# A new order of the same 1519 steps in a one-core chain of four convolution blocks

## Chip, cores and metric

The kernel runs on one core of a Trainium2 chip. The metric is the device time of one execution in microseconds (us); lower is better. Besides TensorE (PE), VectorE (DVE), ScalarE (ACT), GpSimd (POOL) and SyncE (SP) the core has 16 DMA engines.

## What is computed

Four blocks follow each other on an input x of 4 images, 512 channels, 32x32 pixels, all in fp32:

```
# L0: deformable bottleneck
out    = relu(bn1(conv1x1(x)))                     # 512 -> 128
offset = conv3x3(out) + off_b                      # 18 values for each pixel
out    = relu(bn2(deform_conv3x3(out, offset)))    # 9 taps, 4 corners each, bilinear
x      = relu(bn3(conv1x1(out)) + x)               # 128 -> 512
# L1: local self correlation, 5x5 window, normalised, beside x
gs     = l2norm(sum_c x[y+dy, x+dx] * x[y, x])     # 25 values for each pixel
x      = relu(W @ concat(x, gs) + b)
# L2, L3: two residual bottlenecks (1x1 to 128, 3x3, 1x1 to 512, plus x, relu)
```

## The kernel before

**Tiling.** An image has 1024 pixels. It is worked in two halves `h` of 512 pixels, which is one bank of PSUM, and the 512 channels in four groups `m` of 128. The deformable convolution of one image is 18 units `u` (2 halves x 9 taps). A unit has 4 tiles of 128 pixels and is cut in two parts `q` of two tiles.

**The path of a unit.** `gather.i.u.q` issues two indirect DMAs on POOL (L572), each of which fetches for 128 pixels the four corner pixels (128 x 512 floats, 256 KB) from a table in HBM into one of 12 `patch` slots. Behind each DMA POOL waits for its own last `tick` and adds a single number to itself (L577); this is the pause behind each gather. `weigh` (ACT, L860) multiplies the first corner, `blend` (DVE, L1130) adds the other three in six instructions, `turn` (PE, L694) transposes the four tiles, `sampT` (ACT, L868) copies them out of PSUM, and `tap` (PE, L705) multiplies by the weights of the tap. A gather may only start when the blend of three units before has emptied its slots. After nine taps come `hid` (ACT), four `out0` (PE, L713), and `xsum`, `xhigh`, `xlow` (DVE, ACT, DVE), which make the sum with x, and its split into a high and a low part. `res` on SP loads x for `xsum` into two buffers.

**What goes before.** `conv1`, `mid`, `taps`, `tapped`, `shift` and `positions` make the offsets, the addresses and the weights of an image; `midT`, `pixels` and `table` write its table. `stage`, `split`, `splitlow`, `scale`, `turnw`, `w3turn`, `w3scale` and their like prepare the weights of the later blocks.

**What comes behind.** L1 is `gram` (PE, 24 matmuls of 256 columns), `copies` (ACT), `win`, `norm` (DVE), `corrT` (PE, L732), `gsT`, `gslow`, `mixA` and `mixB` (PE, L749), `mixhigh`, `mixlow`. L2 and L3 (the third number of a step is 2 or 3) are `red`, `cvA` and `cvB`, `ex`, each followed by a `val`, a `high` (ACT) and a `low` (DVE) step, and at the end `final` and `store`. These matmuls are made as three products each (L596 to L598, the function `product`).

**What sets the order.** The string `ORDER` lists all steps. Every engine walks it from the front, and issues the steps that are its own, in this order and no other. All waits are counted from it too: `nth(step)` is how often a kind has been reached, and a wait is always for the number that its producer has in the string. `assign` walks the same string to give five PSUM banks (`take` waits until the last user has returned one) and four `ring` slots. So a moved step changes the place of its instructions on its engine, and, with the banks, what a later step waits for, but not what it computes. An order keeps `turn`s of image 3 among the L2 and L3 matmuls of image 2, and so on; behind `turn.3.17`, the last, only image 3's own L1, L2 and L3 and what is left of image 2 are to be done.

Of the kernel before, what the change touches and what calls it, by code (L numbers as in the profile page):

```python
# [1238 lines left out]
```

## Time and profile before

| | |
|---|---|
| median of three runs | 678.51 us (675.9 to 679.7) |
| the profiled execution | 670.66 us, span of its core 668.9 us |
| busy: PE, DVE, POOL, ACT | 586.6, 436.1, 400.1, 321.5 us |
| mean granted TensorE clock | 0.949 |
| moved by DMA | 110.07 MB, 75.52 MB of it by the gathers |

The span is the time from the first to the last instruction of the core. A busy time is the sum of what the records of an engine cover. Matmuls of PE overlap each other, so that the sum of their durations is more than the time they take; the time that a step takes is read from the distance of starts. "Granted clock" is the share of full speed (2.4 GHz) that TensorE was given; it is either 1.0 or 0.5 (1.2 GHz) at a time.

### The profile page before, as it was taken

How to read it: one execution, taken by the hardware profiler on the slowest of the kernel's cores; microseconds unless marked ns; L12 is line 12 of the kernel's file. 1: busy time of each engine (PE TensorE's matmuls, PEld its weight loads, DVE VectorE, ACT ScalarE, POOL GpSimd, SP SyncE). 2: the span in 40 equal slices, each digit the busy share in tenths (PEclk: the TensorE clock that was granted, in tenths of full speed). 3: DMA queues.
4: the chain of work that ended last, by engine and by line, in shares of the span. 5: the costliest groups of instructions: out<-in, count | busy, mean ns of one | idle time of the engine just before them, and what ended most of it. 6: DMA issues, size and time to landing. Idle time of an engine off the chain costs nothing.

```text
span 668.9 us, 8597 instructions
## 1 busy us (share of the span) xinstructions
PE 586.6 (88%) x2568; PEld 427.8 (64%) x2568; DVE 436.1 (65%) x1288; ACT 321.5 (48%) x702; POOL 400.1 (60%) x598
## 2 busy tenths in 40 slices
PE   6966876346979899999999899997999899999997
PEld 2654563133767677657777675574877675888776
DVE  3236668576869688788894765894876577473222
ACT  2233445434445476554542864643356745423533
POOL 2287757888684787886878486875269851000000
PEclk9978979658889999999999999996999999999999
DMA  8797963875552655785656358764054645200003
GB/s 290 239 361 248 317 175 111 236 235 142 158 164 88 177 162 170 247 267 193 175 145 189 90 159 266 235 219 144 27 162 127 172 129 172 63 1 1 0 1 125
DMA packets 47984, 110.07 MB, mean 165 GB/s; under 512 B 7607, under 2 KB 15863, under 8 KB 47810
## 3 DMA queue, kind: packets, MB, share of 16 engines
q0 software_dynamic: 23040, 75.52, 38.0%
q1 hardware_dynamic: 24898, 34.00, 15.2%
q8 instruction: 21, 0.34, 0.2%
q14 instruction: 25, 0.20, 0.1%
HBM read 96.94 MB, written 12.55 MB: 164 GB/s over the span
## 4 chain that ended last, share of the span: by engine, by line
PE 44%; DVE 17%; POOL 12%; DMA 8%; issue 8%; ACT 6%; another core or an unknown queue 4%; SPq 0%; ACTq 0%; DVEq 0%; POOLq 0%
PE bank L596 10%; PE bank L598 10%; PE bank L597 9%; DVE samp L1130 9%; POOL patch L572 9%; PE bank L705 4%; POOL tick L577 3%; PE bank L630 3%; PE bank L779 2%; DMA res<-in_x 2%; DMA patch<-patch_table,idx_all 2%; DMA patch<-patch_tables,idx_all 2%; PE bank L694 2%; PE bank L713 1%
## 5 line engine op out<-in xcount | busy, mean ns | idle before, releaser
L572 POOL DMA_INDIRECT patch<-patch_tables,idx_all x216 | 234.5, 1086 | 94.3 <-DVE samp L1130 63.5
L1130 DVE SCALAR_TENSOR_TENSOR samp<-patch,wgt_all,samp 128x128 f32<-128x128 f32 x864 | 236.7, 345 | 72.9 <-ACT samp L860 57.8
L860 ACT ACTIVATE samp<-patch,wgt_all 128x128 f32<-128x128 f32 x288 | 98.1, 394 | 86.3 <-PE bank L694 36.5
L572 POOL DMA_INDIRECT patch<-patch_table,idx_all x72 | 74.2, 1030 | 49.3 <-DVE idx_all L1037 24.1
L577 POOL TENSOR_TENSOR tick<-tick 1x1 f32<-1x1 f32 x288 | 85.6, 297 | 5.3
L705 PE MATMUL bank<-sampT,w 128*128 128x512 f32 x144 | 77.4, 640 | 8.3 <-ACT sampT L868 5.9
L694 PE MATMUL bank<-ident_r,samp 128*128 128x128 f32 x288 | 45.8, 286 | 27.1 <-DVE samp L1130 24.3
L694 PEld LDWEIGHTS bank<-ident_r,samp 128*128 128x128 f32 x288 | 35.8, 146 | 48.7 <-DVE samp L1130 34.9
L596 PE MATMUL bank<-x_high,l1w_high 128*128 128x512 f32 x128 | 55.5, 434 | 0.1
L868 ACT ACTIVATE sampT<-bank 128x512 f32<-128x512 f32 x72 | 42.0, 589 | 23.8 <-PE bank L694 11.5
L598 PE MATMUL bank<-x_high,l1w_low 128*128 128x512 f32 x128 | 50.7, 396 | 0.0
L597 PE MATMUL bank<-x_low,l1w_high 128*128 128x512 f32 x128 | 50.6, 396 | 0.0
L596 PE MATMUL bank<-x_high 128*128 128x256 f32 x128 | 40.1, 314 | 7.9 <-issue 6.1
L705 PEld LDWEIGHTS bank<-sampT,w 128*128 128x128 f32 x144 | 26.6, 204 | 26.0 <-issue 15.1
L598 PE MATMUL bank<-x_high,x_low 128*128 128x256 f32 x128 | 38.0, 297 | 2.1 <-issue 2.0
L1136 DVE SCALAR_TENSOR_TENSOR res<-bank,prm,res 128x512 f32<-128x512 f32 x32 | 23.6, 746 | 24.6 <-DMA res<-in_x 12.6
L713 PE MATMUL bank<-hid,w 128*128 128x512 f32 x64 | 34.4, 643 | 5.9 <-issue 3.3
L879 ACT ACTIVATE x_high<-res 128x512 fp32r<-128x512 f32 x32 | 20.0, 627 | 40.4 <-DVE res L1136 34.9
L597 PE MATMUL bank<-x_low,x_high 128*128 128x256 f32 x128 | 38.0, 297 | 0.3 <-issue 0.3
L630 PE MATMUL bank<-xa,w 128*128 128x512 f32 x64 | 32.5, 658 | 6.0 <-DMA xa<-in_x 6.0
L893 ACT ACTIVATE corr<-bank 32x320 f32<-32x320 f32 x64 | 27.4, 428 | 20.0 <-remote 11.1
L779 PE MATMUL bank<-xs_high,ident_r 128*128 128x512 f32 x64 | 32.1, 501 | 4.7 <-DVE h_low L1172 3.9
(178 smaller groups left out, 1165.0 us busy)
## 6 DMA issues: line engine op xcount, KB each, us to landing
res<-in_x SPq DMA_DIRECT2D x32, 256.0 KB
out_y<-ring SPq DMA_DIRECT2D x32, 256.0 KB
xa<-in_x SPq DMA_DIRECT2D x7, 1024.0 KB, 5.4
patch<-patch_tables,idx_all POOLq DMA_INDIRECT x216
patch_tables<-midT SPq DMA_DIRECT2D x11, 256.0 KB
patch<-patch_table,idx_all POOLq DMA_INDIRECT x72
xa<-in_x SPq DMA_DIRECT2D x4, 256.0 KB, 5.7
xa<-in_l1wt SPq DMA_DIRECT2D x1, 1024.0 KB
```

Source lines behind the costliest of these rows:

```text
L572: pool.indirect_dma_start(patch[:, n % SLOTS].rearrange("p a c -> p (a c)"), None, patches_n if i else patches_0, bass.IndirectOffsetOnAxi ...
L577: pool.tensor_tensor(tick[:, 1:2], tick[:, 0:1], tick[:, 0:1], ALU.add).then_inc(ticked, 1)
L596: pe.matmul(ps, w[0], a[0], start=start, stop=False)
L597: pe.matmul(ps, w[0], a[1], start=False, stop=False)
L598: return pe.matmul(ps, w[1], a[0], start=False, stop=stop)
L630: last = pe.matmul(ps[:], w1[:, c, :], xa[i % 2][:, c, h * HALF:(h + 1) * HALF], start=c == 0, stop=c == KC - 1)
L694: last = pe.transpose(bank[TURN_BANK + u % 2][:, t * P:(t + 1) * P], samp[:, u % 2, t, :], ident)
L705: pe.matmul(bank[TAP_BANK][:], w2[:, k, :], sampT[:, u % 2, :], start=k == 0, stop=k == TAPS - 1).then_inc(tap_done, 1)
L779: pe.matmul(ps[:], ident_r[:], xs[p][:, m, h * HALF:(h + 1) * HALF], start=p == 0, stop=False)
L860: act.activation(samp[:, u % 2, t, :], patch[:, g % SLOTS, 0, :], ACT.Copy, scale=wgt_all[:, i, (HT * h + t) * TAPS + k, 0:1]).then_inc(we ...
L868: act.activation(sampT[:, u % 2, :], bank[TURN_BANK + u % 2][:], ACT.Copy).then_inc(sampT_done, 1)
L1130: dve.scalar_tensor_tensor(o_, g_, w_, o_, ALU.mult, ALU.add).then_inc(blended, 1)
```

## The change

The string `ORDER` is replaced by another order of the same 1519 steps. No other line is changed: no instruction is added or removed, and the pause behind each gather is there before and after. Of the steps in their engines' sequences, 55 of 412 of PE, 54 of 383 of DVE, 68 of 501 of ACT and 138 of 145 of POOL stand at the same place. Below are both orders from the front to `turn.0.17`, and both places of `turn.3.17`.

```diff
-shift.0 table.0.1 midT.0.0 positions.0 conv1.1.0 pixels.0.0 table.0.0 mid.1.0 gather.0.0.0 taps.1.0 xload.2.0
-conv1.1.1 midT.1.0 gather.0.0.1 mid.1.1 gather.0.1.0 tapped.1.0 midT.1.1 taps.1.1 taps.1.2 gather.0.1.1 xload.2.1
-tapped.1.1 weigh.0.1.0 pixels.1.0 weigh.0.0.0 blend.0.0.0 blend.0.1.0 gather.0.2.0 conv1.2.0 mid.2.0 tapped.1.2
-pixels.1.1 gather.0.2.1 midT.2.0 shift.1 weigh.0.0.1 weigh.0.1.1 blend.0.0.1 blend.0.1.1 pixels.2.0 xload.3.0
-res.0.0.0 gather.0.3.0 positions.1 turn.0.0 taps.2.0 weigh.0.2.1 sampT.0.0 tapped.2.0 gather.0.3.1 conv1.2.1 xload.3.1
-gather.0.4.0 tap.0.0 weigh.0.2.0 mid.2.1 taps.2.1 midT.2.1 turn.0.1 weigh.0.3.0 gather.0.4.1 blend.0.2.0 blend.0.3.0
-blend.0.2.1 turn.0.2 gather.0.5.0 conv1.3.1 table.1.1 stage.0 table.2.0 weigh.0.4.0 gather.0.5.1 weigh.0.3.1 sampT.0.1
-blend.0.4.0 blend.0.3.1 tap.0.1 turn.0.3 gather.0.6.0 weigh.0.5.0 blend.0.5.0 w3turn w3scale sampT.0.2 pixels.2.1
-sampT.0.3 gather.0.6.1 conv1.3.0 w3back tap.0.2 weigh.0.5.1 weigh.0.4.1 blend.0.5.1 blend.0.4.1 scale.0 gather.0.7.0
-w3s scale.1 tap.0.3 turn.0.4 turn.0.5 sampT.0.4 weigh.0.6.1 tapped.2.1 gather.0.7.1 taps.2.2 tapped.2.2 weigh.0.7.0
-weigh.0.6.0 shift.2 blend.0.6.1 blend.0.6.0 table.1.0 stage.1 res.0.0.1 split.2 mid.3.0 gather.0.8.0 mid.3.1
-gather.0.8.1 positions.2 taps.3.0 turn.0.6 taps.3.1 turnw.1 taps.3.2 tap.0.4 gather.0.9.0 weigh.0.8.0 sampT.0.5
-tap.0.5 tapped.3.2 split.1 sampT.0.6 tapped.3.1 blend.0.8.0 gather.0.9.1 blend.0.7.0 tapped.3.0 weigh.0.8.1
-weigh.0.7.1 turnw.0 tap.0.6 shift.3 midT.3.0 split.4 blend.0.8.1 blend.0.7.1 gather.0.10.0 positions.3 gather.0.10.1
-turn.0.7 weigh.0.9.1 weigh.0.9.0 sampT.0.7 turn.0.8 tap.0.7 sampT.0.8 gather.0.11.0 tap.0.8 pixels.3.0 split.5
-blend.0.9.1 blend.0.9.0 weigh.0.10.1 gather.0.11.1 split.3 hid.0.0 weigh.0.10.0 blend.0.10.1 blend.0.10.0 out0.0.0.0
-gather.0.12.0 out0.0.0.1 turn.0.9 xsum.0.0.1 weigh.0.11.0 sampT.0.9 splitlow.3 xsum.0.0.0 gather.0.12.1 xhigh.0.0.1
-out0.0.0.3 tap.0.9 midT.3.1 turn.0.10 blend.0.11.0 xlow.0.0.1 gather.0.13.0 res.0.0.3 table.3.0 sampT.0.10
-weigh.0.12.0 blend.0.12.0 corrw xhigh.0.0.0 out0.0.0.2 weigh.0.11.1 gather.0.13.1 weigh.0.12.1 pixels.3.1 split.0
-blend.0.11.1 splitlow.4 xsum.0.0.3 splitlow.0 xlow.0.0.0 blend.0.12.1 gather.0.14.0 turn.0.11 res.0.0.2 table.3.1
-table.2.1 sampT.0.11 weigh.0.13.1 xsum.0.0.2 splitlow.1 gather.0.14.1 tap.0.10 turn.0.12 xhigh.0.0.3 weigh.0.14.0
-weigh.0.13.0 split.6 blend.0.13.1 gather.0.15.0 blend.0.13.0 xhigh.0.0.2 xlow.0.0.2 xlow.0.0.3 tap.0.11 turn.0.13
-splitlow.6 blend.0.14.0 splitlow.5 gather.0.15.1 weigh.0.14.1 weigh.0.15.0 gather.0.16.0 blend.0.15.0 res.0.1.1
-gram.0.0 res.0.1.0 gather.0.16.1 blend.0.14.1 sampT.0.13 sampT.0.12 weigh.0.15.1 blend.0.15.1 gather.0.17.0 tap.0.12
-tap.0.13 turn.0.14 splitlow.2 turn.0.15 weigh.0.16.1 sampT.0.14 gather.0.17.1 sampT.0.15 weigh.0.16.0 blend.0.16.1
-blend.0.16.0 tap.0.14 tap.0.15 weigh.0.17.0 mixA.0.0.0 gather.1.0.0 blend.0.17.0 weigh.0.17.1 turn.0.16 blend.0.17.1
-gather.1.0.1 sampT.0.16 tap.0.16 turn.0.17 sampT.0.17 weigh.1.0.0 tap.0.17 gather.1.1.0 blend.1.0.0 hid.0.1 out0.0.1.0
...
-weigh.3.17.1 sampT.3.14 tap.3.13 final.2.1.0 turn.3.16 tap.3.14 sampT.3.15 blend.3.17.1 store.2.1.0 tap.3.15
-sampT.3.16 xlow.3.0.3 turn.3.17 tap.3.16 sampT.3.17 res.3.1.1 res.3.1.0 tap.3.17 ex.2.3.1.3 hid.3.1 out0.3.1.1
-final.2.1.3 out0.3.1.0 store.2.1.3 xsum.3.1.1 ex.2.3.1.1 xhigh.3.1.1 xsum.3.1.0 xlow.3.1.1 xhigh.3.1.0 out0.3.1.3
...
+shift.0 table.0.1 midT.0.0 positions.0 pixels.0.0 table.0.0 gather.0.0.0 xload.2.0 conv1.1.1 gather.0.0.1 conv1.1.0
+gather.0.1.0 xload.2.1 conv1.2.0 gather.0.1.1 weigh.0.0.1 mid.1.1 mid.1.0 weigh.0.0.0 taps.1.0 blend.0.0.0
+gather.0.2.0 taps.1.2 midT.1.0 taps.1.1 blend.0.0.1 gather.0.2.1 weigh.0.1.1 tapped.1.1 tapped.1.0 turn.0.0 conv1.2.1
+tapped.1.2 pixels.1.0 xload.3.0 table.1.0 weigh.0.1.0 gather.0.3.0 blend.0.1.1 blend.0.1.0 weigh.0.2.0 midT.1.1
+turn.0.1 shift.1 gather.0.3.1 blend.0.2.0 sampT.0.0 mid.2.0 weigh.0.2.1 mid.2.1 blend.0.2.1 gather.0.4.0 taps.2.2
+taps.2.1 tap.0.0 midT.2.1 positions.1 xload.3.1 turn.0.2 gather.0.4.1 pixels.1.1 tapped.2.1 weigh.0.3.1 pixels.2.1
+sampT.0.2 weigh.0.3.0 gather.0.5.0 blend.0.3.0 blend.0.3.1 conv1.3.0 gather.0.5.1 weigh.0.4.0 weigh.0.4.1 sampT.0.1
+blend.0.4.1 blend.0.4.0 turn.0.3 tap.0.1 taps.2.0 gather.0.6.0 sampT.0.3 weigh.0.5.1 weigh.0.5.0 tapped.2.0 midT.2.0
+turn.0.4 conv1.3.1 gather.0.6.1 tapped.2.2 mid.3.0 gather.0.7.0 blend.0.5.0 blend.0.5.1 tap.0.2 shift.2 w3turn
+turn.0.5 weigh.0.6.1 mid.3.1 gather.0.7.1 sampT.0.4 taps.3.1 taps.3.2 gather.0.8.0 res.0.0.0 stage.0 stage.1 table.1.1
+pixels.2.0 weigh.0.6.0 blend.0.6.0 blend.0.6.1 taps.3.0 turn.0.6 positions.2 res.0.0.1 gather.0.8.1 tap.0.3
+weigh.0.7.1 weigh.0.7.0 w3scale weigh.0.8.0 gather.0.9.0 weigh.0.8.1 split.5 sampT.0.5 blend.0.7.0 tapped.3.2
+gather.0.9.1 blend.0.7.1 split.3 tap.0.4 turn.0.7 gather.0.10.0 tap.0.5 blend.0.8.0 weigh.0.9.1 sampT.0.6 tapped.3.1
+split.2 gather.0.10.1 splitlow.5 blend.0.8.1 tapped.3.0 weigh.0.9.0 w3back turn.0.8 shift.3 midT.3.1 gather.0.11.0
+blend.0.9.1 scale.0 blend.0.9.0 sampT.0.7 weigh.0.10.0 gather.0.11.1 weigh.0.10.1 turn.0.9 tap.0.6 tap.0.7 sampT.0.8
+weigh.0.11.1 blend.0.10.1 turnw.0 gather.0.12.0 weigh.0.11.0 w3s blend.0.10.0 turn.0.10 midT.3.0 tap.0.8 positions.3
+gather.0.12.1 sampT.0.9 hid.0.0 weigh.0.12.0 gather.0.13.0 weigh.0.12.1 blend.0.11.1 blend.0.11.0 out0.0.0.0
+out0.0.0.1 blend.0.12.0 gather.0.13.1 corrw sampT.0.10 xsum.0.0.1 blend.0.12.1 gather.0.14.0 turn.0.11 tap.0.9
+xsum.0.0.0 scale.1 out0.0.0.3 out0.0.0.2 gather.0.14.1 xhigh.0.0.0 turn.0.12 tap.0.10 xlow.0.0.0 pixels.3.1
+xhigh.0.0.1 split.0 weigh.0.13.0 blend.0.13.0 res.0.0.2 sampT.0.11 weigh.0.13.1 gather.0.15.0 weigh.0.14.1
+weigh.0.14.0 xlow.0.0.1 blend.0.13.1 tap.0.11 turn.0.13 blend.0.14.0 xsum.0.0.2 table.2.0 res.0.0.3 gather.0.15.1
+xhigh.0.0.2 split.4 weigh.0.15.0 gather.0.16.0 xsum.0.0.3 sampT.0.12 sampT.0.13 tap.0.12 blend.0.14.1 pixels.3.0
+weigh.0.15.1 table.3.0 gather.0.16.1 blend.0.15.0 xlow.0.0.2 tap.0.13 turn.0.14 table.3.1 table.2.1 splitlow.4
+blend.0.15.1 gather.0.17.0 turn.0.15 turnw.1 sampT.0.14 weigh.0.16.1 weigh.0.16.0 gather.0.17.1 blend.0.16.1
+blend.0.16.0 sampT.0.15 turn.0.16 tap.0.14 tap.0.15 xhigh.0.0.3 split.1 weigh.0.17.0 splitlow.1 blend.0.17.0
+gather.1.0.0 split.6 weigh.0.17.1 blend.0.17.1 gather.1.0.1 sampT.0.16 corrlow splitlow.0 turn.0.17 tap.0.16
...
+sampT.3.14 weigh.3.16.1 xsum.3.0.2 xhigh.3.0.3 sampT.3.15 weigh.3.17.1 blend.3.16.1 weigh.3.17.0 cvB.2.3.0
+blend.3.17.1 blend.3.17.0 cvB.2.3.1 turn.3.17 cvval.2.3.0 turn.3.16 cvhigh.2.3.0 tap.3.14 cvlow.2.3.0 xlow.3.0.3
+tap.3.15 cvval.2.3.1 ex.2.3.0.0 cvhigh.2.3.1 cvlow.2.3.1 ex.2.3.0.2 xhigh.3.0.2 sampT.3.16 tap.3.16 sampT.3.17
...
```

## Rows read from the trace of the kernel before

**Rows 1.** The page: span, and busy time with share and instructions of each engine.
```profile
span 668.9 us, 8597 instructions
PE 586.6 (88%) x2568; PEld 427.8 (64%) x2568; DVE 436.1 (65%) x1288; ACT 321.5 (48%) x702; POOL 400.1 (60%) x598
```

**Rows 2.** Stretches: length, PE, PEld, DVE, ACT, POOL busy, clock, DMA, GB/s.
```profile
28.70:162.20 133.50, 87.05 (x362) 57.98 (x361) 87.02 (x297) 54.29 (x128) 106.19 (x151) 0.83 0.74 235
162.20:564.00 401.80, 377.19 (x1659) 276.79 (x1658) 299.37 (x869) 219.32 (x493) 290.14 (x428) 0.97 0.56 169
564.00:668.90 104.90, 100.75 (x466) 79.81 (x464) 39.39 (x68) 39.69 (x70) 0.00 (x0) 1.00 0.10 36
```

**Rows 3.** Timeline (start, us, what, idle before) of PE: two turns.
```profile
123.69 1.11 PE L694 MATMUL bank<-ident_r,samp 128*128 128x128 f32 x4 [6.54 <-DVE samp L1130]
...
563.13 0.66 PE L694 MATMUL bank<-ident_r,samp 128*128 128x128 f32 x4
```

**Rows 4.** Timeline of PE: two products of 512 columns, and `corrT.0.0`.
```profile
435.84 0.40 PE L596 MATMUL bank<-x_high,l1w_high 128*128 128x512 f32 x1
436.08 0.39 PE L597 MATMUL bank<-x_low,l1w_high 128*128 128x512 f32 x1
...
195.77 0.92 PE L732 MATMUL bank<-ident_r,gs 128*96 128x128 f32 x4 [3.42 <-issue]
```

**Rows 5.** Chain of work that ended last: a landing, and two taps.
```profile
35.55 6.19 DMA patch<-patch_table,idx_all
...
513.77 1.72 PE bank L705 x4
```

**Rows 6.** Timeline of POOL: gathers, and one slow tick.
```profile
28.75 1.14 POOL L572 DMA_INDIRECT patch<-patch_table,idx_all  x1 [24.11 <-DVE idx_all L1037]
...
66.36 0.97 POOL L572 DMA_INDIRECT patch<-patch_table,idx_all  x1
...
110.44 3.72 POOL L572 DMA_INDIRECT patch<-patch_table,idx_all  x1 [2.31 <-DVE samp L1130]
...
125.75 0.97 POOL L572 DMA_INDIRECT patch<-patch_table,idx_all  x1
127.07 0.97 POOL L572 DMA_INDIRECT patch<-patch_table,idx_all  x1
...
148.64 4.51 POOL L577 TENSOR_TENSOR tick<-tick 1x1 f32<-1x1 f32 x1
...
554.02 0.97 POOL L572 DMA_INDIRECT patch<-patch_tables,idx_all  x1
```

**Rows 7.** Timeline of DVE: the first four blends; first and last instruction of `positions.1`.
```profile
43.16 6.41 DVE L1130 SCALAR_TENSOR_TENSOR samp<-patch,wgt_all,samp 128x128 f32<-128x128 f32 x24 [15.30 <-ACT samp L860]
...
50.83 0.31 DVE L1012 TENSOR_TENSOR pos<-bank,offb_t 128x144 f32<-128x144 f32 x1 [1.26 <-PE bank L664]
...
55.71 0.38 DVE L1037 TENSOR_SCALAR idx_all<-entry 128x72 int32<-128x72 f32 x1
```

**Rows 8.** Groups of DVE: `splitlow.6`, `xlow` (count, busy us, mean ns, idle).
```profile
L1109 DVE TENSOR_TENSOR l1w_low<-xa,l1w_high 128x2048 fp32r<-128x2048 f32 x1 | 2.3, 2285 | 0.0
L1143 DVE SCALAR_TENSOR_TENSOR x_low<-res,x_high 128x512 fp32r<-128x512 f32 x32 | 21.8, 688 | 7.2 <-ACT x_high L879 6.8
```

**Rows 9.** Waits: who waited for whom, us in total, times, longest.
```profile
POOL patch L572 <- DVE samp L1130: 79.2, 24, 17.9
...
ACT samp L860 <- PE bank L694: 36.5, 14, 7.6
```

**Rows 10.** Timeline of PE, ACT and DVE: pauses without a releaser on the core.
```profile
452.69 0.28 PE L598 MATMUL bank<-x_high,x_low 128*128 128x256 f32 x1 [0.96 <-issue]
...
369.51 0.78 ACT L928 ACTIVATE ring<-bank,bn 128x512 f32<-128x512 f32 x1 [10.53 <-remote]
...
415.04 0.75 DVE L1136 SCALAR_TENSOR_TENSOR res<-bank,prm,res 128x512 f32<-128x512 f32 x1 [6.44 <-remote]
```

**Rows 11.** Busy time of the stretch around the first (columns as in rows 2).
```profile
447.00:462.00 15.00, 10.76 (x61) 9.10 (x59) 9.33 (x25) 4.49 (x12) 13.32 (x22) 0.78 0.75 227
```

More of the change, by code:

```diff
@@ new lines @@
+weigh.1.0.1 gram.0.0 gather.1.1.1 blend.1.0.0 hid.0.1 blend.1.0.1 weigh.1.1.0 gather.1.2.0 out0.0.1.1 out0.0.1.0
+blend.1.1.0 out0.0.1.2 turn.1.0 gather.1.2.1 out0.0.1.3 xsum.0.1.1 xhigh.0.1.1 xsum.0.1.0 xlow.0.1.1 xhigh.0.1.0
+sampT.1.0 res.0.1.3 xlow.0.1.0 gather.1.3.0 weigh.1.2.0 weigh.1.1.1 res.0.1.2 blend.1.1.1 mixA.0.0.3 mixA.0.0.0
+weigh.1.2.1 xsum.0.1.3 gather.1.3.1 xhigh.0.1.3 xsum.0.1.2 tap.1.0 xlow.0.1.3 xhigh.0.1.2 turn.1.1 res.1.0.1
+xlow.0.1.2 blend.1.2.1 blend.1.2.0 borders gram.0.1 res.1.0.0 weigh.1.3.0 weigh.1.3.1 gather.1.4.0 copies.0.0
@@ new lines @@
+blend.2.1.0 res.1.1.0 gram.1.0 cvval.0.3.1 gather.2.3.0 hid.1.1 weigh.2.2.0 cvhigh.0.3.1 blend.2.1.1 cvlow.0.3.1
+weigh.2.2.1 ex.0.3.0.0 out0.1.1.0 blend.2.2.1 gather.2.3.1 out0.1.1.1 copies.1.0 blend.2.2.0 ex.0.3.1.3 ex.0.3.1.0
+final.0.0.0 sampT.2.0 gather.2.4.0 xsum.1.1.0 store.0.0.0 xsum.1.1.1 xhigh.1.1.0 turn.2.2 ex.0.3.1.1 xlow.1.1.0
+xhigh.1.1.1 final.0.1.3 res.1.1.2 out0.1.1.2 turn.2.1 xlow.1.1.1 gather.2.4.1 store.0.1.3 final.0.1.0 res.1.1.3
+out0.1.1.3 store.0.1.0 final.0.1.1 tap.2.0 ex.0.3.1.2 mixA.1.0.1 weigh.2.4.0 store.0.1.1 sampT.2.1 xsum.1.1.2
@@ new lines @@
+gather.2.5.0 xhigh.1.1.2 weigh.2.3.0 xsum.1.1.3 xlow.1.1.2 xhigh.1.1.3 weigh.2.4.1 xlow.1.1.3 gather.2.5.1 weigh.2.3.1
+res.2.0.0 res.2.0.1 gram.1.1 final.0.1.2 store.0.1.2 gram.1.2 blend.2.4.0 blend.2.3.0 blend.2.3.1 blend.2.4.1
+gather.2.6.0 copies.1.1 turn.2.3 mixA.1.0.3 gram.1.3 win.1.0.0 win.1.0.1 gather.2.6.1 copies.1.2 weigh.2.5.0
+weigh.2.5.1 win.1.0.2 mixA.1.0.0 win.1.0.3 gather.2.7.0 root.1.0 copies.1.3 sampT.2.2 norm.1.0 gather.2.7.1
+blend.2.5.0 corrT.1.0 tap.2.1 win.1.1.0 mixA.1.0.2 win.1.1.1 gather.2.8.0 gsT.1.0 gslow.1.0 mixB.1.0.0 mixB.1.0.1
@@ new lines @@
+final.1.1.3 res.2.1.2 sampT.3.0 xlow.2.1.1 store.1.1.3 blend.3.2.0 res.2.1.3 mixA.2.0.3 gather.3.5.0 xsum.2.1.2
+xhigh.2.1.2 xsum.2.1.3 turn.3.2 xlow.2.1.2 xhigh.2.1.3 weigh.3.3.0 tap.3.0 gather.3.5.1 res.3.0.0 xlow.2.1.3 tap.3.1
+blend.3.3.0 gram.2.1 weigh.3.4.0 weigh.3.3.1 blend.3.4.0 gather.3.6.0 weigh.3.4.1 copies.2.0 blend.3.3.1 gram.2.2
+blend.3.4.1 gather.3.6.1 copies.2.1 turn.3.3 gram.2.3 win.2.0.0 gather.3.7.0 win.2.0.1 sampT.3.3 copies.2.2 sampT.3.2
+win.2.0.2 mixA.2.0.0 mixA.2.0.2 win.2.0.3 gather.3.7.1 root.2.0 copies.2.3 norm.2.0 win.2.1.0 weigh.3.5.0 corrT.2.0
```

225 lines of the change are left out of this document (103 added, 122 removed).

## Prediction

> **What bounds the kernel now.** I read the page first, then the busy time by stretch, then the waits, and then the timelines of PE and POOL at the places where PE is idle. The page says PE 88%, and no other engine over 65% [rows 1]. That is an average over three different stages, and the stretches show them [rows 2].
>
> From 28.7 to 162.2 us, image 0 is gathered. PE is busy 87 of 133.5 us there, at 0.83 of full speed. POOL is busy 106 us, DVE 87. PE has all of its early matmuls done and waits for blends: `turn.0.11` came after 6.5 us of idle time that DVE's blend ended [rows 3]. So the gathers, and the blends that free their slots, set the pace of this stage. From 162.2 to 564 us PE is busy for 377 of 402 us, while DVE has 299 and POOL 290 [rows 2]: this stage is bound by PE. Behind `turn.3.17` at 563.1 us [rows 3] POOL is done, and PE is busy 100.8 of 104.9 us.
>
> Hence this way to count: the time is what PE has to do at full clock, plus what it loses. Where PE isn't interrupted a product of 512 columns follows the last after 0.235 us [rows 4], one of 256 columns after half of that, a `tap` takes 0.86 us (two taps in 1.72 us [rows 5]) and a `turn` half of a tap, since its four matmuls have 512 columns together and a tap's two have 1024. All PE steps of `ORDER`, counted so, are 548 us. The span is 669, so 121 us are lost: 6 before the first matmul, some 68 more by `tap.0.17` at 165 us, some 40 from there to `turn.3.17`, and a few in the tail. Only the losses can change, since both orders have the same 548 us.
>
> **Part 1: image 0 is gathered sooner.** The bounds first. The first gather is at 28.75 us and gathers follow each other after 1.32 us [rows 6]. The 72 of image 0 can't take less than 95 us, so the last is issued by 124 at the earliest; with a landing (6.2 us [rows 5]), a weigh and a blend (6 instructions in 1.6 us [rows 7]) `turn.0.17` can't start before some 131. Before, it starts at 161.6. DVE gives a like bound: it blends from 43.2 us on [rows 7], and with its 87 us of busy time in this stage [rows 2] that is 130.
>
> I walked through the new order by hand with durations of these rows. Four things in it make it shorter. ACT does `weigh.0.0.1` first, whose gather lands 2.6 us before the one that the old order waits for first, so the first slots come free about 1.5 us sooner. `positions.1` (50.8 to 56.1 us, after a wait for PE [rows 7]) stood ahead of `blend.0.2.0`, with all blends behind it; now both blends of unit 2 are ahead of it. `gather.0.6.0` comes at 61 us in this walk, against 66.4 [rows 6]. `positions.2` and `positions.3` don't bring new delays, since both move a unit or two back, and `gather.0.12.0` comes at 94 against 110.4 [rows 6]. Last, five DVE steps (`splitlow.0`, `.2`, `.3`, `.6` and `xlow.0.0.3`, 2.3 us for `splitlow.6`, 0.7 for a step of 512 columns [rows 8] of which three are, and 1.3 for `splitlow.3` with 1152, between the two: 5.7 us together) move from ahead of `blend.0.17.1` to behind it. The walk ends with `turn.0.17` at 138.
>
> It is too good, since it has no slow records of POOL. Before, nine records of the gather and the tick in this stage are over 0.5 us longer than usual, 16 us in all (one of 3.7 and one of 4.5 us stand in [rows 6]); all start while DVE works without a gap. Nothing in the new order puts gaps into DVE. I add 9 us of these 16, because some of them fall where POOL would have waited anyway. That gives 147 us, 15 sooner, between the ends of 131 (31 sooner) and 162 (none).
>
> The Trainium skill (SBUF — State Buffer, SBUF: two separate sides) says that DVE and GpSimd share a pair of ports, and that who comes second waits until the other's instruction ends. By that a slow record would be at most one DVE instruction longer, and nothing would be added to the walk. The 4.51 us tick [rows 6] lies beside 15 DVE instructions that follow each other, so here the loser waits for a gap, not for one instruction; I go by the row.
>
> **Part 2: PE has less to fill the wait with.** Ahead of `turn.0.17` the old order has three PE steps that the new one puts behind it: `gram.0.0` (24 x 0.12 = 2.9 us), `mixA.0.0.0` (12 x 0.235 = 2.8 us) and `tap.0.16` (0.9 us). These 6.5 us used idle time of PE before; now they come on top of what is behind. The stage is worth 15 - 6.5 = 8.5 us. Its ends are 31 - 6.5 = 24.5 us of gain, and 6.5 us of loss where the gathers come no sooner. The same holds further back: six `ex`, a turn and two taps stood ahead of `turn.3.17` (6 x 5 x 0.235 + 0.44 + 2 x 0.86 = 9.1 us) and stand behind it now. So the new order is right only if the last blend comes 9.1 us sooner, for nothing, and at 544 rather than 563 for the whole gain. DVE and POOL were busy for 299 and 290 of 402 us in the middle stage [rows 2], so they have the room, and a gather starts as soon as slots are free: POOL waited 79 us for blends [rows 9].
>
> **Part 3: PE's consumers stand further from it.** ACT waited 36.5 us for turns [rows 9], and these waits pass on to the blends behind them. I compared, for each pair of PE steps that an ACT or DVE step joins, the PE work between them with the chain's length (a `sampT` of 0.6 us and its semaphores, 0.95 together, for turn to tap). Before, 12 of 72 taps have less than that, 3.6 us short together; now 2, 0.2 us short. Most of these are in image 0 and so in part 1 already. Where PE bounds, the clear case is `corrT.0.0`, before which PE was idle for 3.4 us [rows 4]: between the last `gram` and it stand 10.7 us of PE work, not 9.4, which takes off 1.3 us. The bank waits are as far off as before (8.1 against 8.0 us of PE work on average). I count 1.5 us for all of this, between 0 and 5.
>
> **Part 4: the rest costs nothing by the rows.** The order of gathers is all but the same (138 of 145 steps of POOL). SP issues the two `stage`s together and later, and `table.1.1` behind them; image 1's table is wanted only 60 us later, and that is its cover. If it were gone it would be the landing of 3.3 MB, 14 us at the 235 GB/s of this stage [rows 2]. The tail has the same distances as before, and I count it at its 104.9 us plus the 9.1 us that moved.
>
> **The sum.** 670.7 of the profiled execution - 8.5 - 1.5 = 660.7 us. The median of the runs shown is 7.8 us over that execution (678.5 against 670.7), and I carry the difference over: 668.5, say 669 us, 1.4% less.
>
> **The rivals.**
>
> *Pauses of an engine without a releaser (slower).* From 452 to 463 us PE runs two or three matmuls at a time with pauses between (the first in [rows 10]), and loses 9.1 us in one `gram`; this falls into a stretch in which POOL issues one gather after the other (13.3 of 15 us busy [rows 11]), and ends with it. ACT at 369.5 and DVE at 415.0 start again 1.3 and 0.3 us behind the end of two other such runs of gathers, after 10.5 and 6.4 us [rows 10]. That looks like an engine that gets no new instructions while gathers hold the DMA engines; the trace doesn't show it as such. If it is that, an order that gathers faster makes more of it. A pause that hits PE costs 9.1 us: with one more the new order has 669.8 in the profile, nothing gained; it decides from two more on, which give 678.9, that is 687. For it: in my walk POOL has two runs of 21 us in image 0. Against: such runs were there before (12 gathers from 110 on, without a pause of PE's). Chance 0.2.
>
> The Trainium skill (Runtime: NRT & Kernel Launch, Instruction fetch mechanics) says that a sequencer fetches its instructions by a DMA queue of its own ahead of need, and that this is mostly hidden. By that this rival would be worth nothing. The rows don't agree with it if the pauses are fetches, and I keep the rival.
>
> *The gain is given back (no change).* The last blend comes sooner, but only by the 6.5 to 9.1 us that the moved PE work needs, because weighs and blends in the middle stage stand as close to what they wait for as before (a turn of images 1 to 3 starts mostly 1 to 2 us behind its last blend). Then the profile shows 670 and the median 678. Chance 0.2.
>
> *The walk holds.* No slow POOL records, and `turn.0.17` at 138: 9 us less than forecast, 660. Chance 0.12.
>
> **How the numbers follow.** The forecast (fewer losses in image 0, kept to the end) has 0.48, with a range of its own of 663 to 675; the three rivals have 0.2, 0.2 and 0.12. 8 times in 10 the time should be between 657 and 685: that takes in the walk that holds but for its end, no change, and the pauses up to nearly two. What this kernel's measurement can tell from no change is about 0.5%, or 3.4 us. Faster by more than that: the forecast and the walk, less 0.01 of the forecast that lies above 675, is 0.59. Slower: the pauses, and 0.02 of the gain given back, where it is more than that, is 0.22. Within it is the rest, 0.19.
>
> **What would show it.** In the profile of the changed kernel `turn.0.17` starts near 147 us, and PE is busy for less than 87 us before it; the last gather is issued near 535 and not 554 [rows 6], and `turn.3.17` starts near 544. If `turn.0.17` is early and `turn.3.17` isn't, the gain was given back, and the rows between them show idle PE behind DVE or with no releaser. If `turn.0.17` is not before 155, part 1 is wrong. Any pause of PE beyond the one at 452 us, in a full run of gathers, speaks for the first rival.

## The result, and the profile after

The changed kernel takes 684.0 us (median of 20 runs, 673.2 to 696.0), the old one beside it 680.3 us (20 runs, 662.9 to 695.4). The ratio is 1.0145 with a 95% interval of [1.0083, 1.0208]; it is taken over undisturbed runs alone, and leans on the fastest of the old kernel's 20, 662.9 us, which stands 12 us below the next. So the 1.4% that was forecast isn't there: by medians the new order is 0.5% slower, by the ratio 0.8 to 2.1%, and that it is slower at all is less sure than that it gains nothing. The time lies inside the forecast range of 657 to 685.

The profiled execution of the new order took 686.5 us. First its page, then the three stretches (length, then busy time of PE, PEld, DVE, ACT and POOL, granted clock, DMA share, GB/s), which answer to rows 1 and 2:

```profile
span 684.7 us, 8597 instructions
PE 588.9 (86%) x2568; PEld 429.9 (63%) x2568; DVE 435.8 (64%) x1288; ACT 318.3 (46%) x702; POOL 393.9 (58%) x598
```

```profile
28.70:162.20 133.50, 75.72 (x304) 46.55 (x302) 74.23 (x268) 49.33 (x120) 97.63 (x147) 0.81 0.71 223
162.20:564.00 401.80, 374.18 (x1647) 278.07 (x1648) 305.20 (x886) 215.07 (x491) 291.58 (x432) 0.95 0.56 168
564.00:668.90 104.90, 104.53 (x484) 82.72 (x484) 41.63 (x78) 40.91 (x72) 0.00 (x0) 1.00 0.09 31
```

The page alone tells little: each engine is busy for as long as before. The first stretch tells where: in the same 133.5 us PE did 76 us of work and not 87, DVE 74 and not 87, POOL 98 and not 106 [rows 2]. All engines got less done there, and no engine more. So something holds all of them.

The waits of after (who waited for whom: us in total, times, longest) name it:

```profile
POOL patch L572 <- DVE samp L1130: 97.0, 29, 16.9
...
ACT samp L860 <- remote: 27.1, 5, 11.8
...
ACT sampT L868 <- remote: 19.9, 4, 7.1
...
ACT tapped L820 <- remote: 14.9, 2, 9.4
...
DVE pos L1012 <- remote: 12.6, 2, 7.4
ACT corr L893 <- remote: 12.3, 2, 9.8
```

"remote" is a wait for which no releaser shows on the core: it ends with a record of the semaphore that comes over 1.5 us behind the end of every instruction that raises it. In the trace of before these sum to 43 us, the longest two 10.5 and 6.4 us [rows 10]; in after to 106 us. POOL's wait for blends grew from 79.2 us [rows 9] to 97.0, behind them. Such waits are the pauses of what follows; a doubled or tripled pause is always the one behind each gather.

The timeline of ACT in after shows the first of them:

```profile
39.83 1.38 ACT L860 ACTIVATE samp<-patch,wgt_all 128x128 f32<-128x128 f32 x4
50.61 0.57 ACT L820 ACTIVATE tapped<-bank 128x486 f32<-128x486 f32 x1 [9.39 <-remote]
```

`tapped.1.1` waits for the last of three groups of PE's matmuls (L648). The timeline of PE shows it, and that PE then waits in turn:

```profile
43.57 0.99 PE L648 MATMUL bank<-offw,mid 128*128 128x162 f32 x6
44.40 0.60 PE L694 MATMUL bank<-ident_r,samp 128*128 128x128 f32 x4
51.33 6.53 PE L630 MATMUL bank<-xa,w 128*128 128x512 f32 x8 [6.33 <-ACT tapped L820]
```

All of `tapped.1.1`'s input was there at 44.6 us, and ACT, with nothing else in its queue, started at 50.6. The next places are `positions.2`, ready at 91.8 and started at 99.2, and `copies.1.0`, ready at 313.2 and started at 323.0.

The way to read on is a table of milestones, start times in us, with the span's last instruction. The last two columns are the same two orders on another chip (the first two experiments below):

```
                     before   after | old again  new again
gather.0.6.0           66.4    73.2 |    66.0      61.9
gather.0.12.0         110.4   124.9 |   106.9     108.2
turn.0.17             161.5   169.7 |   158.2     148.8
last gather           552.7   557.2 |   532.3     506.1
turn.3.17             563.1   570.2 |   542.7     519.2
last instruction ends 666.4   682.2 |   645.7     631.3
```

(`last gather` is the first of the two DMAs of the last gather step.) From before to after: 8.2 us later at `turn.0.17`, 1.1 us won back up to `turn.3.17`, and 8.7 us more behind it. On the other chip: 9.4 us sooner, 14.1 us more won, and 9.1 us more behind `turn.3.17`. The last difference is the same on both, and is the PE work that was moved there. The rest changes sign with the chip. (The two profiled executions of the first chip are 15.8 us apart, the medians only 3.7: that of before was one of its faster ones.)

### The profile page after: what moved, and what is told of

The parts are those of the page before. It is cut to its first block, busy times and chain, and to the rows that moved or that the text cites. A ratio compares the mean times of both kernels' runs of the same rounds, so it can differ in the third digit from the quotient of the medians.

```text
span 684.7 us, 8597 instructions
## 1 busy us (share of the span) xinstructions
PE 588.9 (86%) x2568; PEld 429.9 (63%) x2568; DVE 435.8 (64%) x1288; ACT 318.3 (46%) x702; POOL 393.9 (58%) x598
## 4 chain that ended last, share of the span: by engine, by line
PE 64%; another core or an unknown queue 8%; issue 7%; POOL 6%; ACT 5%; DVE 5%; DMA 4%; SPq 0%; ACTq 0%; DVEq 0%; POOLq 0%
PE bank L596 15%; PE bank L598 14%; PE bank L597 14%; PE bank L705 7%; POOL patch L572 5%; PE bank L779 4%; PE bank L694 3%; PE bank L713 3%; DMA patch<-patch_table,idx_all 3%; ACT samp L860 2%; DVE samp L1130 2%; PE bank L630 1%; POOL tick L577 1%; PE bank L749 1%
## 5 line engine op out<-in xcount | busy, mean ns | idle before, releaser
L572 POOL DMA_INDIRECT patch<-patch_tables,idx_all x216 | 226.8, 1050 | 105.4 <-DVE samp L1130 75.9
L860 ACT ACTIVATE samp<-patch,wgt_all 128x128 f32<-128x128 f32 x288 | 95.8, 394 | 85.2 <-DMA patch<-patch_table,idx_all 36.4
L572 POOL DMA_INDIRECT patch<-patch_table,idx_all x72 | 78.7, 1093 | 54.3 <-DVE idx_all L1037 23.2
L705 PE MATMUL bank<-sampT,w 128*128 128x512 f32 x144 | 81.0, 670 | 12.3 <-issue 12.3
L577 POOL TENSOR_TENSOR tick<-tick 1x1 f32<-1x1 f32 x288 | 82.6, 287 | 5.3
L694 PE MATMUL bank<-ident_r,samp 128*128 128x128 f32 x288 | 47.8, 294 | 32.5 <-DVE samp L1130 28.2
L694 PEld LDWEIGHTS bank<-ident_r,samp 128*128 128x128 f32 x288 | 37.8, 151 | 57.4 <-DVE samp L1130 39.6
L596 PE MATMUL bank<-x_high 128*128 128x256 f32 x128 | 37.2, 291 | 4.9 <-issue 2.6
L597 PE MATMUL bank<-x_low,x_high 128*128 128x256 f32 x128 | 36.3, 284 | 0.0
L1172 DVE TENSOR_TENSOR h_low<-ring,h_high 128x512 fp32r<-128x512 f32 x16 | 11.0, 691 | 38.1 <-ACT h_high L933 26.6
```

The lines of the kernel that those rows point to most:

```text
L572: pool.indirect_dma_start(patch[:, n % SLOTS].rearrange("p a c -> p (a c)"), None, patches_n if i else patches_0, bass.IndirectOffsetOnAxi ...
L577: pool.tensor_tensor(tick[:, 1:2], tick[:, 0:1], tick[:, 0:1], ALU.add).then_inc(ticked, 1)
L596: pe.matmul(ps, w[0], a[0], start=start, stop=False)
L597: pe.matmul(ps, w[0], a[1], start=False, stop=False)
L694: last = pe.transpose(bank[TURN_BANK + u % 2][:, t * P:(t + 1) * P], samp[:, u % 2, t, :], ident)
L705: pe.matmul(bank[TAP_BANK][:], w2[:, k, :], sampT[:, u % 2, :], start=k == 0, stop=k == TAPS - 1).then_inc(tap_done, 1)
```

## The experiments

Each call of runs went to one chip, with the old kernel timed beside it. I call the five chips of the experiments A (the first four), B (the pause and the corners), C (load, taps, positions), D and E; the chip of the result isn't known, and can be one of them. The theories at the start: A, gathers that come faster hold the DMA engines and so bring pauses; B, the waits that the order itself sets make the loss; C, the pauses belong to the chip or the hour, and the new order gains without them.

**1. Both orders again (chip A).** No edit.

> The kernel before, unchanged, for a second trace. Theory A (pauses of ACT and DVE that no engine ends, at the end of long runs of gathers, make the difference and fall where chance puts them): the image 0 stage, read at turn.0.17, differs from the 161.6 us of the first trace by 5 us or more. Theory B (the waits that the order itself sets make it): turn.0.17 within 2 us of 161.6, and the same idle times in the same places.

> The changed kernel, unchanged, for a second trace. Theory A: turn.0.17 moves by 5 us or more from the 169.7 us of its first trace, and the pauses of ACT (11.8 us before weigh.0.7.1) and DVE (7.4 us before positions.2) stand elsewhere or are of another length. Theory B: turn.0.17 again near 170, with the same pauses. Ratio to the kernel before: 1.00 to 1.02 by both.

Measured: old order 647.2 and 645.1 us (10 and 19 runs, ratio 1.0009 [0.9950, 1.0067]), new order 635.7 us (4 runs, 626.1 to 645.4; 1.5% under the old by medians, too few runs for a ratio), where both theories had 1.00 to 1.02. No wait without a releaser is in either trace. The old order's `turn.0.17` is at 158.2 us, 3.4 from its first trace, which fits neither A nor B; the new order's moves by 21 us, as A had it. The first two stretches of the new order on this chip:

```profile
28.70:162.20 133.50, 90.38 (x374) 56.63 (x373) 94.60 (x320) 60.55 (x141) 115.52 (x171) 0.86 0.80 254
162.20:564.00 401.80, 393.56 (x1836) 300.74 (x1835) 311.93 (x883) 225.80 (x509) 278.52 (x408) 1.00 0.55 167
```

The same program does 90 us of PE work in the first stretch and not 76. And ACT's timeline at the place of the 6 us pause:

```profile
42.78 0.40 ACT L860 ACTIVATE samp<-patch,wgt_all 128x128 f32<-128x128 f32 x1 [0.25 <-DMA patch<-patch_table,idx_all]
46.13 1.38 ACT L820 ACTIVATE tapped<-bank 128x486 f32<-128x486 f32 x3 [2.95 <-PE bank L648]
47.38 0.62 ACT L811 ACTIVATE midT<-bank 128x512 f32<-128x512 f32 x1
```

`tapped.1.1` starts 0.04 us behind PE's `taps`, with a releaser named. Old and new differ here as forecast, by sign and size of the whole.

**2. Where the gain is without pauses (chip A).** The order cut at the end of image 0 and joined the other way round:

```
e3: ORDER = old order up to weigh.0.17.0, then the new order's remaining steps
e4: ORDER = new order up to turn.0.17, then the old order's remaining steps
```

> The old order up to weigh.0.17.0, which is all of image 0's gathering, and behind it the remaining steps in the new order. If the loss is made in image 0 (by A or B), this is within 0.5% of the kernel before or faster, and turn.0.17 stands near 162. If it is made in the middle stage, it is 1% or more slower, as the changed kernel is.

> The new order up to turn.0.17, and behind it the remaining steps in the old order. If the loss is made in image 0, this is 1% or more slower than the kernel before, with turn.0.17 near 170. If it is made in the middle stage, it is within 0.5% of the kernel before.

Measured: e3 636.7 us, ratio 0.9871 [0.9801, 0.9941]; e4 641.7 us, 0.9975 [0.9927, 1.0023]. The loss that the two were to place isn't there on this chip; they place the gain. With the new order for image 0 alone `turn.0.17` is 7.5 us sooner (150.7 against 158.2), but nothing of it can be told from zero at the end. With the new order behind image 0 alone nearly all of the gain is there. By the loss of PE (start of a turn less PE's work ahead of it at full clock) old and new again stand at 69.3 and 66.4 us at `turn.0.17`, but at 87.1 and 71.6 at `turn.1.17`. So of 15.5 us of loss saved there (14.4 at the end) 2.9 are made in image 0 and 12.6 in image 1's stretch. Single traces of one order differ by as much: the old order's steps bring `turn.0.17` at 158.2 us in e1, 153.6 in e3 and 155.1 in e11, and `turn.1.17` differs by up to 12 us. In image 1's stretch the old order loses some 18 us in e1 but 12 to 13 in e4, e11 and e12, the new one 5 in e2 and 11 in e3 (worked out in the same way). So this split has e3's and e4's medians for its proof, not the traces, and 12.6 us is its high end.

**3. The pause behind each gather taken away (chip B).**

```
-                        pool.wait_ge(ticked, ticks[0] + 1)
-                        pool.tensor_tensor(tick[:, 1:2], tick[:, 0:1], tick[:, 0:1], ALU.add).then_inc(ticked, 1)
-                        ticks[0] += 1
```

> The old order with the pause behind each gather (the wait for the last tick and the new tick) left out, so that gathers are issued about 1.0 us apart rather than 1.32. Theory A (engines without new work are held up while gathers come one behind the other): waits that nothing on the core ends, of 5 us and more, appear for ACT, DVE or PE, 20 us or more in all, and the kernel is slower than with the pause although its gathers are issued sooner. Theory C (such waits belong to the chip and not to the gathers): no such waits, and the kernel is as fast or faster.

Measured: 646.8 us, ratio 1.0089 [1.0043, 1.0136], no wait without a releaser. Gathers back to back don't bring the pauses on this chip. For the new order without the tick there is no result.

**4. Half of the gathers' bytes (chips B and E).** Each gather fetches two of its four corners; the two others are left out of the blend (zeros stand in their place, cleared once at the start).

```
-  pool.indirect_dma_start(patch[:, n % SLOTS].rearrange(...), None,
+  pool.indirect_dma_start(patch[:, n % SLOTS, 0:2].rearrange(...), None,
```

> The old order with gathers that fetch only two of the four corners, so half the bytes, at the same count and pace; the other half of the slots is cleared once at the start, so that corners 2 and 3 add nothing. If the load on the DMA engines matters, gathers land sooner: the landing waits of ACT go from some 45 us to under 20 and turn.0.17 comes at 150 or sooner instead of 158. If it is DVE and the order's waits alone, turn.0.17 stays at 156 to 160.

> The new order with half the bytes to each gather, as in the last one. With the load of the DMA engines taken away the new order should keep turn.0.17 at 9 us or more ahead of the old one, if what it gains in image 0 comes from the places of weighs and positions; if it came from landings, the two are within 3 us.

> New order with one pause, each gather fetching two of the four corners (the two others are left out of the blend's sum as zeros): half the bytes, as many gathers and as many increments by them. One look. On a chip with late increments: if their number follows the gathers' count, over 100 of ACT's increments are late as before; if it follows bytes or packets, under 60 are. On a chip without, none, and 615 to 620 us.

Measured: old order 628.8 us, new order 617.3 us and, against the old kernel's 641.2, 0.9600 [0.9503, 0.9697]; on chip E 624.7 in one run beside 645.6, above the 615 to 620 expected. For the old order the bytes are worth 12 us, and the two orders stay 1.8% apart with half of them; `turn.0.17` is at 145.2 and 137.4 us, 7.8 apart, between the two answers that e8 was to choose from. No chip with pauses was met, so the question put to e19 (count or bytes) stays open.

**5. More load on the DMA engines (chip C).** Three copies of `x`, 8 MB each, from HBM to HBM, ahead of `pixels.0.1`:

```
+  act.dma_start(echo[c].ap()..., x...).then_inc(echoed, 16)     # c in range(3)
```

> The old order with three copies of x from HBM to HBM (8 MB each, 24 MB read and 24 MB written) issued from ACT at some 19 us, ahead of pixels.0.1, so that the DMA engines have other traffic during image 0. It computes the same. Theory A (the pauses of the first two traces are engines that get nothing new while DMA engines are taken): waits of ACT, DVE or PE that nothing on the core ends come back, 20 us or more in all, and stand in the stretch of the copies. Theory C (a state of that chip that DMA traffic doesn't make): no such waits, only later landings.

> The new order with the same three copies. If the new order is the more sensitive to late landings (its waits of ACT on gathers were 66 us against 45), its lead of some 9 us at turn.0.17 shrinks to under 5 or turns; if it isn't, turn.0.17 stays 9 us or more ahead of the old order with the copies.

Measured: 714.2 us (1.1117 [1.0985, 1.1248]) and 696.9 us (1.0880 [1.0781, 1.0980]), with the DMA engines 96% busy from 20 to 150 us, and not one wait without a releaser. Load of this sort doesn't bring them on a chip that has none. Theory A falls in the form it had; on a chip with pauses load wasn't tried.

**6. Two steps of the old order by themselves (chip C).**

```
e11: tap.1.1 and tap.1.2 moved ahead of corrT.0.0
e12: positions.1 moved behind blend.0.2.1
```

> The old order with tap.1.1 and tap.1.2 moved ahead of corrT.0.0, two PE steps of 0.86 us, and nothing else. If PE waits for corrT.0.0 because too little work stands between the grams and it, the 3.2 us gap before it shrinks by 1.7 us or more, the taps behind it no longer run at half clock (0.85 us), and the kernel gains 2 to 4 us (0.3 to 0.6%). If the step is late for another reason that moves with it, the gap stays.

> The old order with positions.1 moved behind blend.0.2.1 (from ahead of blend.0.2.0), and nothing else. By my prediction's part 1 blend.0.2.0 comes 3 us or more sooner and gather.0.6.0 follows at some 63 us instead of 66; turn.0.17 comes 1 to 4 us sooner if that is kept. If something else sets the pace in between, gather.0.6.0 moves and turn.0.17 stays at 158.

Measured: 641.0 us, 0.9975 [0.9923, 1.0027], and 645.0 us, 1.0018 [0.9955, 1.0082]. The gap before `corrT.0.0` goes from 3.2 us to nothing, and 1.5 us of it comes back one step on. `gather.0.6.0` comes 1.6 us sooner in e12 (64.4, against 66.0 in e1; 65.1 in e11), but the old order's own steps gave 64.2 in e3. `turn.0.17` is at 150.6 in e12, against 155.1 in e11, from one trace each. By their medians neither can be told from no change.

**7. The new order, the old one, and a doubled pause (chip D).** This chip is like the first.

```
e15, the new order, behind each gather once more:
+                        pool.wait_ge(ticked, ticks[0] + 1)
+                        pool.tensor_tensor(tick[:, 1:2], tick[:, 0:1], tick[:, 0:1], ALU.add).then_inc(ticked, 1)
+                        ticks[0] += 1
```

> The changed kernel once more, on whatever chip comes. Theory C (the 43 and 106 us of waits without a releaser belong to the chip of the result, and the new order gains where they are absent): no such waits in the trace, turn.0.17 within 146 to 152 us, loss of PE ahead of turn.0.17 near 66 us, time 0.985 to 0.99 of the kernel before beside it. Rival (the new order itself lengthens or shifts them, so that it is slower in general): waits without a releaser of 60 us or more on ACT and DVE, turn.0.17 at 160 us or later, ratio 1.005 to 1.02.

> The old order on the same chip, one look for its trace. Theory C: as many waits without a releaser as in the run of the new order beside it (none if none there), turn.0.17 near 158 us, last product's start near 543 us. Rival: if this chip shows such waits, the new order has at least twice as much of them as the old.

> New order with the pause behind each gather doubled (one more small GpSimd addition and its wait for each gather). Without any pause the old order was 0.9% slower than with one. If the pause helps by spreading GpSimd's accesses out, doubling gives another 0.2 to 0.5% (about 633 us where the new order alone is 636). If it only costs GpSimd time, gathers are issued later by some 0.1 us each, turn.0.17 comes 2 to 6 us later, and the time is 0.3 to 0.9% above the new order's.

Measured: old kernel 686.4 us (23 runs, 666.2 to 697.8), new order 683.4 (12 runs), ratio 1.0168 [1.0078, 1.0258], which rests on two of the old kernel's 23 runs; one run of the old order for its trace, 675.7. Medians and ratio point two ways here, and what stands is that the new order gains nothing. `turn.0.17` is at 167.8 us in the new order and 159.4 in the old, as the rival had it. Doubled pause: 670.1 us (10 runs, 665.1 to 673.8), 0.9894 [0.9818, 0.9970]; beside the new order with one pause it is 13.3 us less, far more than the 0.5% expected at best.

The pauses are back, at the same steps. ACT in the new order on chip D:

```profile
51.26 1.04 ACT L820 ACTIVATE tapped<-bank 128x486 f32<-128x486 f32 x2 [9.12 <-remote]
```

and in its waits and those of the old order beside it:

```profile
ACT samp L860 <- remote: 31.1, 4, 11.8
...
ACT tapped L820 <- remote: 14.7, 2, 9.1
...
ACT corr L893 <- remote: 12.5, 1, 12.5
```

```profile
ACT samp L860 <- remote: 8.3, 3, 6.9
...
ACT ring L916 <- remote: 6.7, 1, 6.7
```

Summed over all such rows they are 96 us in the new order, 44 in the old, as 106 and 43 on the first chip, and none with the doubled pause. On D they are no more in the new order (14 waits, against 16), but longer. Of the 15 that hold ACT or DVE up by over 2 us in after, 10 are at the same step in e13 (`tapped.1.1` by 6.0 us in both, `positions.1` by 4.0 in both, `positions.2` by 7.4 and 5.2, `copies.1.0` by 9.8 and 12.5). The order of steps decides where most of them fall.

**What the pauses are.** Besides instructions the trace records when semaphores change. The records of the semaphores that one engine alone raises, and of the landings of DMAs, are these, with the waits without a releaser beside them:

```
records of                DVE   ACT  POOL    PE  landings | remote, us
before   (first chip)     953   524   182   311      3373 |      43
after    (first chip)     963   529   198   331      3423 |     106
e14 old order     (D)     937   511   191   311      3036 |      44
e13 new order     (D)     967   537   186   320      3243 |      96
e15 new, doubled  (D)    1159   665   576   345      5648 |       0
e1 old order      (A)    1308   721   310   380      6330 |       0
e2 new order      (A)    1308   721   310   380      6331 |       0
e9 old, with load (C)    1308   721   310   380      6376 |       0
```

(With the doubled pause POOL has 288 increments more.) Where there are pauses, a quarter of the engines' records and half of those of landings are missing. A missing record isn't a late increment. POOL shows it: behind each gather it waits for its last tick, and in before 127 ticks have no record within 1 us of their end, but the next tick starts ahead of the semaphore's next record in all 127, and the idle time ahead of all 288 ticks is 5.3 us, as in e1. POOL's own increments reach it in time.

What is late is seen where an engine stands idle until a record comes. Each of the pauses ends so, with the record of the very semaphore that the engine waits for. PE finished `taps.1.1` at 44.56, the record of that semaphore is at 50.58, ACT starts at 50.61. `sampT.1.6`: record at 236.63, ACT starts at 236.65. `redval.0.3.1`: 286.33 and 286.42. `copies.1.0`: 322.93 and 322.96. `positions.2`: 99.07 and 99.17. Sorted by who raised the semaphore, all waits that a record over 1 us late ended are waits of ACT or DVE for PE, 14 in before, 20 in after, 19 in e14 and 17 in e13, but for two in after and two in e13 in which DVE waited for itself; e1, e2 and e15 have none. No wait for ACT or POOL, and none of another engine for DVE, ended so. So ACT and DVE stood ready, and the word from PE came late.

In the time of the first pause (44.6 to 50.55) after has 17 records, 13 of them of landings; e2, which issues the same gathers, has 97, with 64 of landings. POOL issued three gathers and four ticks in it at its usual pace. It looks as if PE's increments stood in line with something of the gathers, and came through at the end of a run of gathers or in a gap of it; that line itself is in no record. Two other readings are as open: that PE itself was held, since the profile models the ends of matmuls and doesn't see them, and that what loses the records also makes the pauses. Why the chip of the result and D do it and A, B, C and E don't, nothing here tells.

**8. The doubled and the tripled tick on a chip without waits of that kind (chip E).** The three lines above added once to the old order and the new one, and twice to the new one.

> Old order with the pause behind each gather doubled. In the traces of the result's chip and of chip 14 hundreds of semaphore increments are recorded over 1 us after their instruction's end (before 131 of DVE's 1290, 152 of ACT's 699, 128 of POOL's 306, 83 of PE's 364), in the four traces of the other chips looked at so far none; with the doubled pause 22, 40, 0 and 31. Theory D (increments queue behind the gathers' own, and room between gathers lets them through): where the kernel before takes 670 us or more, this is 1.5 to 3% faster than it, with under 50 late increments on each engine. Where the kernel before takes about 640 us, no increments are late anyway, and this is within 0.5% of it. Rival (the pause helped the new order alone, by moving its gathers): ratio within 0.5% of 1 on either sort of chip, with 130 or more late increments on ACT where before is slow.

> New order with the doubled pause again, beside the old order with it. Theory D with the forecast's own mechanism (image 0's gathers sooner): 1 to 1.5% faster than the old order with doubled pause, so about 0.96 to 0.975 of the kernel before where that takes 670 us or more, 0.98 to 0.99 where it takes 640. Rival (the new order's dense start keeps its late increments): level with the old order with doubled pause.

> New order with the pause tripled. Theory D: on a chip with late increments the last of them go (under 10 on each engine) and the time is 0 to 0.5% under the doubled pause's. If GpSimd's own time now decides (288 more additions and waits of about 0.21 to 0.29 us each, 60 to 80 us on an engine with some 40 us of idle time left ahead of gathers), 1 to 3% slower than the doubled pause.

Measured, beside 645.6 us for the old kernel: 669.3 us (1.0360 [1.0259, 1.0461]), 669.9 us (1.0357 [1.0298, 1.0416]) and 734.6 us (1.1382 [1.1317, 1.1448]). All three expectations for a chip such as this one were wrong: within 0.5% of the kernel before for e16, e17 1 to 1.5% faster than e16 (they are level, as the rival had it), and e18 at most 3% slower than e17 (it is 9.7%). The chain of work that ended last, share of the span by engine, of e2 with one pause, e17 with two and e18 with three:

```profile
PE 62%; POOL 13%; DVE 9%; DMA 8%; issue 3%; ACT 3%; SPq 1%; ACTq 0%; DVEq 0%; POOLq 0%
```

```profile
POOL 42%; PE 41%; issue 8%; DVE 3%; DMA 3%; ACT 2%; SPq 0%; POOLq 0%; DVEq 0%; ACTq 0%
```

```profile
POOL 66%; PE 15%; issue 13%; DVE 3%; DMA 1%; ACT 1%; SPq 0%; POOLq 0%; DVEq 0%; ACTq 0%
```

and the second pause in the groups of e17 (count, busy us and mean ns, idle us before):

```profile
L580 POOL TENSOR_TENSOR tick<-tick 1x1 f32<-1x1 f32 x288 | 61.9, 215 | 22.6
```

288 pauses take 61.9 + 22.6 = 84.5 us of POOL, and POOL becomes the bound; both orders then take the same, since neither changes how much POOL has to do. The doubled pause takes about 670 us on both sorts of chip. On D that is 2.4% under the old kernel by medians (1.1% by the ratio), on E it is 3.6% over. So no version here beats both kernels everywhere; where there are no pauses e2 and e3 are the fastest of those that compute the whole, at about 636 us. The old order with the doubled pause was never run on a chip with pauses, so that the extra tick helps both orders there isn't shown.

## Why the prediction was wrong

**The bound.** Right: without pauses PE has 62% of the chain that ended last (e2). The count "PE's work at full clock plus what it loses" is a way to keep books and can't fail, since loss is what is left over; it served to place the differences.

**Part 1, image 0 sooner.** `turn.0.17` was forecast at 147 us. Without pauses it came at 148.8, with them at 169.7, which by the part's own test ("not before 155") makes it wrong on the chip of the result. Its steps were right less often than its sum: `gather.0.6.0` at 61.9 (walk 61), but `gather.0.12.0` at 108.2 (walk 94). Two records of POOL between them, 5.30 and 4.99 us for a gather of 0.97, take 8.4 us of the 14. With three smaller ones the new order's slow records come to 12 us in image 0, where the prediction added 9.

```profile
61.95 5.30 POOL L572 DMA_INDIRECT patch<-patch_table,idx_all  x1 [0.75 <-DVE samp L1130]
...
90.27 4.99 POOL L572 DMA_INDIRECT patch<-patch_table,idx_all  x1 [2.97 <-DVE samp L1130]
```

Against the old order on the same chip it was 9.4 us sooner and not 15, since that one too was 3.4 us sooner than on the first chip; and old traces differ by 5 us here.

**Part 2, less to fill the wait.** Right: the stretch behind `turn.3.17` grew by 8.7 and 9.1 us in the two pairs, for 9.1 worked out. But this part took 6.5 us off a gain of 15, and of 9.4 it leaves 2.9: the 8.5 us of the sum were mis-sized by two thirds, and e4 alone shows nothing at the end.

**Part 3, consumers further off.** Mis-sized the other way. Counted at 1.5 us (0 to 5), while e3 has 1.3% (8.4 us by medians) from behind image 0 alone; one pair of traces has 12.6 us of loss saved there. The gap before `corrT.0.0` was real (3.2 us to nothing), but e11 shows that it isn't the gain by itself. Which steps of that stretch make the rest I didn't find.

**The sum.** 1.4% was forecast; without pauses 1.3% (e3) and 1.5% (e2) were measured. That is two errors that cancel: luck, not a right working.

**The first rival.** It happened. It was put at two pauses of 9.1 us or more on PE; what came were pauses of 2 to 12 us on ACT and DVE, which hand them on to POOL (97.0 us of waits for blends) and to PE. The step that failed is the one that set it aside, so that the sum has no term for it: "such runs were there before" was taken for evidence that the order doesn't matter. The runs were, and so were the pauses; but in the new order the waits without a releaser are 106 us and not 43, and on D 96 and not 44. The new order has `tapped.1.1`, `tapped.2.1`, `positions.1` and `positions.2`, all of which wait for PE, inside or right behind runs of gathers in the stage that the gathers bound. That these places make the difference is read off the traces; no run moved one of them on such a chip. In image 0 the old order loses 3.4 us to the chip (161.6 against 158.2) and the new one 20.9 (169.7 against 148.8). From `turn.0.17` to `turn.3.17` it is 17.1 and 30.1. By medians, between chip A and that of the result, the old order loses 35 us and the new one 48: the 13 us between them are the gain and a little more. The rival's cause, an engine without instructions, isn't borne out either: the pauses end with the record of the semaphore that the engine waits for. So the page on instruction fetch that the prediction weighed (the Trainium skill, Runtime: NRT & Kernel Launch, Instruction fetch mechanics) is not contradicted by these pauses.

**The rule on ports.** The 4.51 us tick [rows 6] was laid at DVE's door and not at that of a pause. That holds: the old order has the same tick on chip A (e1), where no wait is without a releaser,

```profile
145.33 4.51 POOL L577 TENSOR_TENSOR tick<-tick 1x1 f32<-1x1 f32 x1
```

and the 3.72 us gather before it as well, at 106.9 us; the two slow gathers of the new order stand in after too. So the slow records go with the order and not with the chip. That DVE makes them was argued from what lies beside them, and no run here tests it.

## What to carry to other kernels

A wait without a releaser on the core is a cost of its own and needs a term in the sum, not a rival with a fifth of the chances: ask which engine stands waiting for PE behind each dense run of indirect DMAs, since that is where the pauses were paid for here, and look whether what is reordered goes into such runs. Whether it helps to keep only work there that needs no other engine wasn't tried. Before a missing record is read as a late one, look whether the engine that waits for it did stand. And have an order that was searched for timed on more than one chip before its 1% is believed; here 1.5% on one chip was nothing or a loss on two others (or one, seen twice).

## What the runs showed of the hardware

- One program takes 636 us on one chip and 684 on another (new order), the other 645 and 680 to 686. The higher times go with waits without a releaser (43 to 106 us), which the traces of the lower ones don't have, and with a quarter of the engines' semaphore records missing (about 2000 of 2719 are there).
- Nearly all the late ends of waits are of ACT and DVE waiting for PE (70 of 74 in four traces). POOL's waits for its own ticks cost 5.3 us on either sort of chip, with 127 of their records missing or with none.
- On such a chip a second addition of 0.21 us and its wait on POOL behind each gather took the waits without a releaser from 96 us to none, and the missing records from 42% of all in the table to 10%. 24 MB of plain copies beside the gathers (DMA engines 96% busy) didn't bring any on a chip that had none.
- Ten of the fifteen pauses over 2 us are at the same steps in the trace of the result and in that of a later call. So the pauses are no noise: they belong to the order of the program and the chip together.
- POOL's slow records belong to the order: 3.72 and 4.51 us in the old one, 5.3 and 5.0 in the new one, each on two chips.
